# The constant's product back on TensorE, the sums' copy on ACT, and half the product of ones

## The reference

```python
# first layer: sum, maximum and mean of the edges of each source node, then a small MLP
seg_sum  = segment_sum(edge_attr, src);  cnt = edges per node
seg_max  = where(cnt > 0, segment_max(edge_attr, src), 0);  seg_mean = seg_sum / max(cnt, 1)
h = relu(concat([seg_sum, seg_max, seg_mean, u[0]]) @ W1 + b1)
x = x + (h @ W2 + b2)
# second layer: normalised rows of the source nodes, summed at the destination nodes
h = relu(layernorm(x))
x = x + relu(segment_sum(h[src], dst) @ W.T + b)
```

## Time and profile before

| what | us |
| --- | --- |
| median of three runs | 1256.63 (1252.74 to 1262.65) |
| the profiled execution | 1261.67 |
| its span | 1259.8 |
| TensorE busy | 960.6 (76%) |
| VectorE busy | 1030.1 (82%) |
| ACT busy | 280.1 (22%) |
| GpSimd busy | 758.0 (60%) |
| mean granted TensorE clock | 0.888 of full speed |

### The profile page before, as it was taken

The page is one execution under the profiler, slowest core; times in us unless marked ns, Lnnn a source line. Parts: engine busy times, 40 slices in busy tenths (PEclk is TensorE's granted clock), DMA queues, the critical chain, the costliest instruction groups (busy, mean ns, idle before and its releaser), DMA issues.

```text
span 1259.8 us, 20767 instructions
## 1 busy us (share of the span) xinstructions
PE 960.6 (76%) x5818; PEld 758.0 (60%) x5818; DVE 1030.1 (82%) x2727; ACT 280.1 (22%) x681; POOL 758.0 (60%) x821
## 2 busy tenths in 40 slices
PE   0131027979999999999999823879889788888888
PEld 0010014757777777777777613767767677677777
DVE  8888887899999999999999624777777777777774
ACT  1441042212222222222222101112112112111110
POOL 3000046667777777777776067777777777777750
PEclk9995556889999999999999955898999989988899
DMA  2000012767899888888888654777788778777775
GB/s 65 0 0 0 0 53 68 175 161 206 236 232 240 234 226 219 241 220 236 230 222 240 164 173 98 180 201 203 210 222 207 202 198 210 210 208 201 203 186 156
DMA packets 317563, 218.51 MB, mean 173 GB/s; under 512 B 223428, under 2 KB 255140, under 8 KB 317444
## 3 DMA queue, kind: packets, MB, share of 16 engines
q1 hardware_dynamic: 182100, 135.41, 38.7%
q10 hardware_dynamic: 110256, 62.42, 18.8%
q0 software_dynamic: 25088, 19.32, 8.6%
HBM read 137.51 MB, written 79.45 MB: 172 GB/s over the span
## 4 chain that ended last, share of the span: by engine, by line
DVE 36%; POOL 20%; DMA 13%; PE 11%; issue 10%; ACTq 5%; ACT 2%; SPq 0%; POOLq 0%; DVEq 0%
POOL xa L559 11%; POOL xa L540 9%; DMA xa<-node_table,gi 8%; DMA win<-records 5%; DVE feats L1074 4%; DVE feats L1072 4%; ACTq L667 3%; DVE oneh L1095 3%; DVE dout L1114 2%; PE p_m L1367 2%; DVE kb L920 2%; DVE ka L920 2%; DVE shared L1095 2%; DVE ka L921 2%; DVE kb L921 2%
## 5 line engine op out<-in xcount | busy, mean ns | idle before, releaser
L540 POOL DMA_INDIRECT xa<-in_edge_attr_dram,gi x392 | 375.2, 957 | 252.3 <-issue 115.4
L559 POOL DMA_INDIRECT xa<-node_table,gi x392 | 369.9, 944 | 158.7 <-issue 105.8
L677 ACT ACTIVATE hid<-p_z,bias_z 128x512 f32<-128x512 f32 x98 | 113.4, 1157 | 249.2 <-issue 230.0
L1408 PE MATMUL p_g<-ident,hn 128*128 128x128 f32 x196 | 46.6, 325 | 106.9 <-DVE hn L1182 106.5
L1074 DVE TENSOR_TENSOR_SCAN feats<-c_rows,feats,p_g 32x512 f32<-32x512 f32 x97 | 123.3, 1271 | 1.4
L1095 DVE SCALAR_TENSOR_TENSOR shared<-p_m,node_of 112x1024 f32<-112x1024 f32 x98 | 117.1, 1195 | 6.8 <-PE p_z L1379 3.4
L1072 DVE TENSOR_TENSOR_SCAN feats<-c_rows,feats,p_g 64x512 f32<-64x512 f32 x97 | 122.5, 1263 | 0.1
L1367 PE MATMUL p_m<-w_s,hid 128*128 128x64 f32 x784 | 109.3, 284 | 15.8 <-ACT hid L677 15.4
L730 ACT ACTIVATE sd<-mv,eps_t 128x4 f32<-128x4 f32 x98 | 29.1, 297 | 413.2 <-DVE mv L1173 350.4
L1095 DVE SCALAR_TENSOR_TENSOR oneh<-p_m,node_of 112x1024 f32<-112x1024 f32 x98 | 119.3, 1217 | 0.2
L1360 PE MATMUL p_z<-feats,w_s 96*128 96x512 f32 x196 | 112.4, 657 | 6.2 <-DVE feats L1074 6.2
(11 more groups left out here) (253 smaller groups left out, 1539.3 us busy)
## 6 DMA issues: line engine op xcount, KB each, us to landing
win<-records SPq DMA_DIRECT2D x980, 28.9 KB
records<-rec ACTq DMA_DIRECT2D x196, 132.0 KB
din<-in_x_dram SPq DMA_DIRECT2D x49, 512.0 KB
node_table<-dout SPq DMA_DIRECT2D x49, 512.0 KB, 3.6
din<-node_table SPq DMA_DIRECT2D x43, 512.0 KB
out_dram<-dout SPq DMA_DIRECT2D x43, 512.0 KB
c_rows<-rows_src ACTq DMA_DIRECT2D x141, 128.0 KB
win<-records ACTq DMA_DIRECT2D x588, 28.9 KB
```

The lines of the kernel that those rows point to most:

```text
L540: g.indirect_dma_start(out=xa[n % XRING][:, t, 0:FE], out_offset=None, in_=edge_attr, in_offset=bass.IndirectOffsetOnAxis(ap=gi[0][:, BT * ...
L559: g.indirect_dma_start(out=xa[k % XRING][:, t, :], out_offset=None, in_=T, in_offset=bass.IndirectOffsetOnAxis(ap=gi[1][:, BT * n + t:BT * ...
L677: s.activation(hid[n % 2][:, :].rearrange("p (t n) -> p n t", n=P), p_z[n % 2][:, :].rearrange("p (n t) -> p n t", t=BT), ACT.Relu, bias=b ...
L1408: last = tr(p_g[n % 2][:, P * h:P * (h + 1)], hn[n % 2][:, 2 * h:2 * h + 2, :].rearrange("p t d -> p (t d)"), ident[:, :])
```

## The change

The first pass no longer subtracts the constant on VectorE (`less_constant` is gone). `layer2` starts each block with a product that writes minus the constant into all 256 columns of `p_m[0]`, and the four products of the second layer add to it. For this the constant is held as three bfloat16 rows whose sum is the float32 value (`three_parts`, a side job of the sort, on VectorE), and multiplied by three rows of ones. ACT then copies the sums into the record as it does in the second pass, and the semaphore `keyed` is gone. `stream` runs over 256 in place of 512 columns in the first pass.

```diff
+        one_b = sb("one_b", [P, P], BF16)
...
+        nc3 = sb("nc3", [P, BT, D], BF16)
...
+            link(g.memset(one_b[:, :], 1.0))
...
             def record(side, n):
                 k = BLOCKS * side + n
                 act.wait_ge(m_ok, k + 1)
-                keys = s.copy(rec[k % RRING][:, :, KEY], rn[side][:, BT * n:BT * (n + 1)])
-                if side == 0:
-                    keys.then_inc(keyed, 1)
-                else:
-                    s.copy(rec[k % RRING][:, :, 0:D], delta(k)).then_inc(copied, 1)
+                s.copy(rec[k % RRING][:, :, KEY], rn[side][:, BT * n:BT * (n + 1)])
+                s.copy(rec[k % RRING][:, :, 0:D], delta(k)).then_inc(copied, 1)
...
             def store_rec(side, n):
                 k = BLOCKS * side + n
-                if side == 0:
-                    act.wait_ge(keyed, k + 1)
                 act.wait_ge(copied, k + 1)
...
+            def three_parts(row, at):
+
+                link(v.tensor_copy(part_b[0][:, :], row[:, :]))
+                link(v.tensor_tensor(part_f[0][:, :], row[:, :], part_b[0][:, :], ALU.subtract))
+                link(v.tensor_copy(part_b[1][:, :], part_f[0][:, :]))
+                link(v.tensor_tensor(part_f[1][:, :], part_f[0][:, :], part_b[1][:, :], ALU.subtract))
+                link(v.tensor_scalar(part_f[1][:, :], part_f[1][:, :], ident[:, at + 2:at + 3], None, ALU.mult))
+                link(v.scalar_tensor_tensor(part_f[2][:, :], part_b[1][:, :], ident[:, at + 1:at + 2], part_f[1][:, :], ALU.mult, ALU.add))
+                link(v.scalar_tensor_tensor(part_f[1][:, :], part_b[0][:, :], ident[:, at + 0:at + 1], part_f[2][:, :], ALU.mult, ALU.add))
+
+            def constant_c():
+
+                three_parts(c_neg, 0)
+                link(v.tensor_copy(nc3[:, :, :], part_f[1][:, :].unsqueeze(1).to_broadcast([P, BT, D])))
...
+                elif t == 8:
+                    constant_c()
...
-            def less_constant(n):
-
-                dve.wait_ge(m_ok, n + 1)
-                v.tensor_tensor(rec[n % RRING][:, :, 0:D], delta(n), c_neg[:, :].unsqueeze(1).to_broadcast([P, BT, D]), ALU.add).then_inc(copied, 1)
...
-                if valid(n - SRC_REC):
-                    less_constant(n - SRC_REC)
...
+                mm(p_m[0][:, 0:BT * D], one_b[0:3, :], nc3[0:3, :, :].rearrange("p q d -> p (q d)"), start=True, stop=False)
                 for t in range(BT):
-                    last = mm(p_m[0][:, D * t:D * (t + 1)], hid[n % 2][:, P * t:P * (t + 1)], w2_s[:, :], start=True, stop=True)
+                    last = mm(p_m[0][:, D * t:D * (t + 1)], hid[n % 2][:, P * t:P * (t + 1)], w2_s[:, :], start=False, stop=t == BT - 1)
...
-                stream(to, BLK)
+                stream(to, BLK if side else BLK // 2)
```

More of the change, by code:

```diff
@@ L132, in build @@
         added_rows = sb("added_rows", [P, D])
-        part_f = sb("part_f", [P, D])
+        nc3 = sb("nc3", [P, BT, D], BF16)
+        part_b = [sb(f"part_b{q}", [P, D], BF16) for q in range(2)]
+        part_f = [sb(f"part_f{q}", [P, D]) for q in range(3)]
         c_bc = sb("c_bc", [P, D])
@@ L265, in build @@
         z_ok, hid_ok, m_ok = sem("z_ok"), sem("hid_ok"), sem("m_ok")
-        copied, keyed = sem("records_copied"), sem("keys_copied")
+        copied = sem("records_copied")
         keys_up = sem("window_keys_in_psum")
@@ L802, in positions @@
                 link(v.tensor_scalar(next_pos[:, :], pos_f[:, :], 1.0, None, ALU.add))
+            def three_parts(row, at):
[9 more added lines that the diff above has]
+                link(v.tensor_copy(nc3[:, :, :], part_f[1][:, :].unsqueeze(1).to_broadcast([P, BT, D])))
             def constant_rows():
-                link(v.tensor_scalar(part_f[:, :], c_bc[:, :], ident[:, CONST[0]:CONST[0] + 1], None, ALU.mult))
-                link(v.scalar_tensor_tensor(added_rows[:, :], b_bc[:, :], ident[:, CONST[1]:CONST[1] + 1], part_f[:, :], ALU.mult, ALU.add))
+                link(v.tensor_scalar(part_f[1][:, :], c_bc[:, :], ident[:, CONST[0]:CONST[0] + 1], None, ALU.mult))
+                link(v.scalar_tensor_tensor(added_rows[:, :], b_bc[:, :], ident[:, CONST[1]:CONST[1] + 1], part_f[1][:, :], ALU.mult, ALU.add))
                 v.tensor_copy(rowmax[:, :], eps_t[:, :]).then_inc(s_wts, 1)
```

## The result

The change makes the kernel **0.4% slower**: 1262.8 us against 1257.9 (medians of 20 runs each), a ratio of 1.004 with a 95% interval of 1.0022 to 1.0057. The forecast was 0.5% faster. The profiled execution of the changed kernel took 1263.09 us, its span 1261.2, against 1261.67 and 1259.8 before: the two traces differ by 1.4 us only, so they are read here for where time moved, and the verdict on the whole comes from the runs.

A forecast was written before the change was run, and what follows sets the result against it. The prediction took GpSimd's gathers, 5.0 us a block, to bound the first pass. Its terms, -4.5 - 1.0 - 2.0 - 0.4 + 1.5 = -6.4 us, gave 1255.3 against the profiled 1261.67, carried over to 1250.2 us; range 1239 to 1266.

The forecast's parts named there:

- It becomes the slowest of the three consumers, but still just keeps GpSimd's pace: First pass: ACT with TensorE takes 4.86 us a block at least, near 5.0 with jolts, against GpSimd's 5.0.
- the ring: First pass: ACT and TensorE waiting on each other, activation through key copy, store and window loads to next activation; 4.86 us forecast.
- the bulk: First pass after 300 us: GpSimd's later waits on the second scan go, -1.0 us (0 to -1.0).
- granted clock still 1.00: TensorE between 300 and 690 us of the first pass: the changed profile would show its clock still full.
- the drain: Behind the first pass's last scans: half a product of ones, 0.43 us, saved on the path, -0.4 us (0 to -1).
- GpSimd is the slowest of the four: First pass: gathers 1.25 us apart, four a block, make GpSimd's 5.0 us a block the slowest of four clocks.
- Slow pairs take 1.38: First pass, ACT's queue: a slow pair of window loads takes 1.38 us, a jolt straight in the ring.
- I take 0.13: TensorE, first pass: the added 256-column product costs 0.13 us a block, bounds 0.11 to 0.33.
- Rival 4: First pass: more idle time on TensorE makes its clock fall, 2 to 20 us on top, 1252 to 1270; chance 0.10.
- The start: First pass before 300 us: eleven subtractions and one cold product of ones saved, -4.5 us (0 to -16.7).
- The sort: Sort ahead of the first pass: eight linked small operations added on VectorE cost +1.5 us (+0.4 to +2.6).
- Rival 3: First pass: the ring of ACT and TensorE passes GpSimd's 5.0 us a block, slower, 1258 to 1265; chance 0.17.

The follow-up runs named there:

- e10: Changed kernel with next activation ahead of window loads, constant's product ahead of its wait, product of ones 256 columns, 512 in the last ten blocks: 1242.9 us, -1.35%.
- e13: e10 with the fourth of each block's four gathers left out from the ninth block on (output wrong): 1225.4 us, -2.67%.
- e14: Changed kernel with the fourth of each block's four gathers left out from the ninth block on (output wrong): 1266.9 us, +0.49%.
- e7: Kernel before, with ACT issuing the next block's activation ahead of the window loads in the first pass: 1250.0 us, -0.69%.
- e1: Changed kernel with the product of ones back at 512 columns, so only the subtraction is moved: 1268.6 us, +0.68%.
- e2: Kernel before, with only the first pass's product of ones halved to 256 columns: 1276.1 us, +1.02%.
- e3: Changed kernel with the constant's product moved ahead of the wait for the hidden layer: 1257.7 us, -0.36%.
- e4: Changed kernel with the product of ones at 512 columns in the first pass's last ten blocks: 1260.5 us, +0.11%.
- e5: Changed kernel with the constant's product ahead of the hidden layer's wait and 512 columns of ones in the last ten blocks: 1249.7 us, -0.89%.
- e9: Changed kernel with next activation ahead of window loads, constant's product ahead of its wait, product of ones 512 columns throughout: 1259.0 us, +0.02%.
- e6: Changed kernel with ACT issuing the next block's activation ahead of the window loads in the first pass: 1244.1 us, -1.15%.
- e8: e1 with the constant's product left out, so the constant is not subtracted and the output differs from the reference's: 1244.3 us, -1.33%.

## Why the prediction was wrong

The step that failed is "It becomes the slowest of the three consumers, but still just keeps GpSimd's pace": the ring's mean turn was 5.15 us and not within 5.0, and the bulk lost 6.3 us where I had a gain of 1.0. The second is "granted clock still 1.00": the drain ran at 1.2 GHz and lost 6.0 us where I had a gain of 0.4. Together they outweigh a start that gained more than forecast.

- **The floor.** "GpSimd is the slowest of the four": true as a floor (e10, e13), wrong as the bound of the kernel (e14). The least turn was nearly right (4.86 forecast, 4.89 measured), but a ring's mean counts: 4.98 in the median and 5.15 with jolts and cold turns. The kernel before was already at 5.05, and e7 gains 0.7% from the ring alone. I had the jolts in hand and added nothing for them. I had also read them too small: "Slow pairs take 1.38", but seven pairs between 300 and 690 us of that trace took longer, up to 1.76.
- **The product's size.** The term "I take 0.13" measured 0.20 in the ring, inside the bounds, and 0.36 on TensorE, beyond the upper bound of 0.33. The estimate came from twelve like products in a row; this one stands alone between groups of another type and size, and the steps on both sides of it grow too. TensorE's block was not 4.53 but 4.76. The Trainium skill, TensorE: Matmul & The Clock Gate, "Back-to-back issue gap", gives a gap between two products from which 256 columns would take 0.11 us, as an estimate; in e1's trace the next product starts 0.21 us after this one.
- **The clock.** Rival 4 had the mechanism, but looked for it in the bulk. There the five slow turns lie 8.0 us above the median in sum; before, three such turns lay 4.5 above theirs. The larger part came in the drain, whose clock I had not looked at. A narrow product of ones makes the fall likelier and is not all of it. Over all executions the mean clock is 0.888 before and 0.871 with the halving alone (e2), 0.881 in the changed kernel and 0.894 with its full width (e1). In the profiles the drain ran at a mean clock of 0.53 to 0.65 with 256 columns in the changed kernel, e2, e3 and e14, and at 0.99 or 1.00 with 512 in e4, e5, e9, e10 and e13. But e1 fell with 512 columns (33.0 us), and e6 did not with 256 (21.5 us).
- **The start** gained 10.7 us and not 4.5. It comes from VectorE: with the subtraction moved alone (e1) the same stage takes 121.0 us, 9.4 less than before, and with the halving alone (e2) 130.2, 0.3 less. Only 2.8 of the 10.7 are won by block 10's last gather (228.4 us), the rest from there to block 22's. Why each of the subtractions is worth more there than its 0.33 us stays open; the granted clock between 234 and 300 us was 0.95 in place of 0.90.
- **The sort** cost 1.7 us (1.5 forecast). VectorE's idle time came to 0.57 us a block (0.4 said), and key copy to store to 0.49, as said.
- **GpSimd and VectorE.** The gathers stayed 1.25 us apart in e8 and e10 with the subtraction gone: no gather was freed. The rule cited from the Trainium skill (SBUF — State Buffer, "Who interferes with whom") had said so, and these traces agree.
- The range, 1239 to 1266, held the time; the sign was wrong. Rival 3, priced at 1258 to 1265, held it too, in part by luck: its ring came with 0.20 us for the product and not 0.33, and about half of the loss was the drain's.

What stays open: how the 0.4% divides between the ring's turns, the bulk's cold turns and the drain, and what besides the width decides whether the drain runs cold. The times vary from execution to execution (the changed kernel's 20 runs span 1257.8 to 1276.6), and single profiles can't apportion that.

## What to carry to other kernels

Follow a wait round until it returns to its own engine: such a ring can bind while every engine of it has idle time, and a slow DMA issue in it delays the whole turn, so move issues that nobody in the ring needs behind the instruction it waits for (here 0.7% in the kernel before, 1.5% in the changed one). A product that seems idle padding can help to hold TensorE's clock: before narrowing it, see where the engine will wait, also in the drain. And price a lone small product by all the steps around it, not by its columns.

## What the hardware showed that was not expected

- A lone 3x256 bfloat16 product between two groups of float32 products took 0.28 us and lengthened TensorE's block by 0.36 us.
- Halving a product whose result nobody reads, with no other edit, made a kernel 1.0% slower, with a mean granted clock of 0.871 over its six executions in place of 0.888 (e2), and of 0.89 in place of 1.00 between 480 and 690 us of its profile.
- In the changed drain TensorE stayed at 1.2 GHz to its end although it was busy for every 5.00 of 5.00 us from 710 to 725 us. In e1, with the wide product of ones, it was just as busy (14.00 of 14.00 us) at 1.2 GHz, and came back to full clock at about 720 us.
